# A deformable-convolution block over 32 images: the preparation of the next image on a new table of units

## The chip, the core and the metric

The kernel runs on one core of a Trainium2 chip. The metric is device time in microseconds (us) of one execution. Five engines run their own instruction streams in the order in which the code writes them: PE (TensorE matmul, with its weight loads shown apart as PEld), DVE (VectorE), ACT (ScalarE), POOL (GpSimd) and SP (SyncE, which here only issues DMAs). They meet at semaphores.

## What is computed

The input is 32 images of 192 channels and 32 x 32 pixels. Each goes through two residual blocks, both with a group normalization (`_gn`, 32 groups) in front. The first block is an attention over channels, the second a deformable 3 x 3 convolution, followed by a batch normalization over all images and a gelu:

```python
qkv = jnp.einsum('bnc,dc->bnd', x_flat, w_qkv)
attn = jax.nn.softmax(jnp.einsum('bcn,bdn->bcd', q, k) * SCALE, axis=-1)
out = jnp.einsum('bnc,dc->bnd', jnp.einsum('bcd,bdn->bcn', attn, v).transpose(0, 2, 1), w_out) + b_out
...
offset = jnp.clip(_conv(x, off_w, off_b), -max_off, max_off)      # max_off = 8
mask = 2.0 * jax.nn.sigmoid(_conv(x, mask_w, mask_b))
p = corner(y0i, x0i, ...) + corner(y0i, x0i + 1, ...) + corner(y0i + 1, x0i, ...) + corner(y0i + 1, x0i + 1, ...)
out = jnp.einsum('bckhw,ock->bohw', p, w.reshape(co, c_, K))
...
yn = (y - mean) * jax.lax.rsqrt(var + 1e-05) * gamma + beta
return jax.nn.gelu(yn, approximate=False)
...
x = x + _L0_conv_ref(_gn(x), ...)
x = x + _L1_conv_ref(_gn(x), ...)
```

## The kernel before

**Main work of an image.** The bilinear sampling is done as matmuls. For a tile of 128 output pixels and one kernel row, POOL multiplies a row hat `ay` by a column hat `bx` into a sampling matrix `sT` (L1324, 24 of them per image in a ring of three buffers). An image has 48 units: 8 tiles, 3 kernel rows, 2 chunks of input rows. In unit u, PE turns the matrix of unit u + 2 (`turn_s`, L680, three transposes into `sps`), multiplies sampled by projected pixels for unit u (`convolve`, L697 to L699, nine matmuls), and projects the input for unit u + 10 (`z_group`, L666 to L670, five matmuls into `zps`). In the last ten units these projections, and in the last two the turns, already belong to the next image, as does what POOL makes for them. ACT copies `sps` and `zps` into 16-bit high parts (`sh`, `zh`), and DVE forms what the copies lose (`sl` at L1147, `zl` at L1141). PE waits for `sl` two units later and cannot run further ahead.

**Preparation of the next image.** After its main work in unit u, each engine calls `part0(u, b + 1)`, a hand-written list that places one piece of the next image's preparation in that unit. In the order of the list: statistics of the loaded image (DVE), group statistics (PE, L532 and L533, four matmuls of two columns), group variance (DVE, L990 to L994), the inverse deviation and bias (POOL, L1290 to L1294), normalization (ACT), residue (DVE, L1000, one instruction per channel block), transposes, the attention by a Gram matrix and its small products (L540 among them), the new `x1`, the second normalization into the planes `x2` with their residues, then the shifted planes `x2s` and the seams `x2w` that wrap round the image (`move`, DVE, L1006 to L1010), the offset convolution (PE, L609, 48 matmuls in each of units 38 and 39) and the hats. The group statistics stand in units 4 and 28, POOL's inverse deviations in 5 and 29, residues in 8, 10, 32 and 34, moves in 33, 35 and 36. POOL has fewer pieces of main work, so it calls the list for units 2p - 4 and 2p - 3 after matrix p.

**Loads and stores.** SP stores the finished `x1` of an image, loads the next `x`, and stores `y`, in that order. After the loop over images there is one pass of batch normalization and gelu over all of `y`, about 230 us, that this change does not touch. The loop runs two images per iteration, so that buffers alternate.

Of the kernel before, what the change touches and what calls it, by code (L numbers as in the profile page):

```python
# [35 lines left out]
P = 128  # L36
C, H, W = 192, 32, 32
N = H * W
# [44 lines left out]
def build(nc, x, w_qkT, w_v, w_outT, b_out, w_off, b_off, w_proj, proj_b, gamma, beta,  # L83
# [6 lines left out]
    with ExitStack() as ctx:  # L90
# [59 lines left out]
        x2s = [sb(f"x2s_{n}", [P, 2, PAD_ROWS * W], F16) for n in ("hi_a", "lo_a", "hilo_b")]  # L150

        x2w = [sb(f"x2w_{n}", [P, 2, 2 * WRAP * W], F16) for n in ("hi_a", "lo_a", "hilo_b")]

        x2 = [sb(f"x2_{n}", [P, 2, PAD_ROWS * W], F16) for n in ("hi_a", "lo_a", "hilo_b")]
# [72 lines left out]
        x1_stored = sem("x1_stored")  # L227
        x2_moved = sem("x2_moved")
# [44 lines left out]
        SLOTS = UNITS  # L273
# [58 lines left out]

        def images(program, eng):

            part0, part1, weights_ready = program
            for u in range(SLOTS):
                part0(u, 0, 0)
                if u == 15:  # L340
                    weights_ready()
            part1(0, 0, True)
            with nc.Fori(1, NB - 2, 2, engines=[eng.engine], hint_back_edge=True) as b:
                part1(b, 1, True)
                part1(b + 1, 0, True)
            part1(NB - 1, (NB - 1) % 2, False)

        def image_alone(program, b, i):

            part0, part1, far_pass = program
            for u in range(SLOTS):
                part0(u, b, 0)
            part1(b, 0, False, i)
            far_pass(b, i)
# [7 lines left out]
        AHEAD = 10  # L364
        FAR_SLOT = S_RING - 1
# [49 lines left out]
        def _(sp):  # L415
# [25 lines left out]

            def convolved(b):
                sp.wait_ge(y_final, b + 1)
                store_y(b)

            attended(0)
            with sp.Fori(1, NB - 2, 2) as b:
                attended(b)
                convolved(b - 1)
                attended(b + 1)  # L450
                convolved(b)
            attended(NB - 1, False)
            convolved(NB - 2)


# [18 lines left out]
            def image(b, i):  # L474
                load_x(i)
                sp.wait_ge(x1_sb, 4 * b + 4)
                store_x1(i)
                sp.wait_ge(y_final, b + 1)
                store_y(i)
# [34 lines left out]
        def _(pe):  # L514
# [29 lines left out]
            def transpose_x(r, b):  # L544
                if r == 0:
                    pe.wait_ge(xn_lo, 4 * b + 2)
# [73 lines left out]
            def part0(u, b, par):  # L620
                if u == 4:
                    group_stats(0, b)
                if 12 <= u < 16:
                    transpose_x(u - 12, b)
                if u == 16:
                    gram_product(b)
                if u == 17:
                    gram_times_wq(b)
                if u == 18:
                    pe.wait_ge(t1_sb, b + 1)  # L630
                    square(log_ps, t1, wk, l0[0], C)
                if u == 21:
                    pe.wait_ge(prob_sb, b + 1)
                    square(r_ps, prob, wo, l0[1], C)
                if u == 22:
# [6 lines left out]
                if 23 <= u < 27:  # L642
                    apply_m(u - 23, b)
                if u == 28:
                    group_stats(1, b)
                if 38 <= u < 40:
                    for t in range(TILES // 2):
                        offset_conv(TILES // 2 * (u - 38) + t, b, par)
# [94 lines left out]
            def part1(b, par, more, i=None):  # L743
# [5 lines left out]
                for u in range(UNITS):  # L749
                    if u + 2 < UNITS:  # L750
                        turn_s(u + 2, b)
                    elif more:
                        turn_s(u + 2 - UNITS, b + 1)
                    convolve(u, b, par)
                    if u == 9 and not more and i is None:
# [3 lines left out]
                    elif more:  # L759
                        z_group(u + AHEAD - UNITS, b + 1, 1 - par)  # L760
                    if u % 12 == 2 and u > 12:
                        turn_y(u // 12 - 1, b)
                    if more:
                        part0(u, b + 1, 1 - par)
                turn_y(3, b)
# [7 lines left out]
        def _(act):  # L773
# [13 lines left out]
            def normalize(as_hi, i, src, hi, n, b):  # L787
# [5 lines left out]
                if i == 0:  # L793
# [3 lines left out]
                    if n or not first(b):  # L797
                        act.wait_ge(xn_lo, 4 * b + 2 * n)
# [7 lines left out]
            def part0(u, b, par):  # L806
                if 6 <= u < 10:
                    i = (u - 6) // 2
                    normalize(u % 2, i, xin, (xh_a, xhl_b)[i][:, :], 0, b)
                if 12 <= u < 16:  # L810
                    r = u - 12
# [4 lines left out]
                if u == 17:  # L816
# [4 lines left out]
                if u == 19:  # L821
# [6 lines left out]
                if u == 21:  # L828
                    act.wait_ge(r_ps, b + 1)
                    copy_blocks(rmat, l0[1], C).then_inc(r_sb, 1)  # L830
                if u == 22:
# [4 lines left out]
                if 30 <= u < 34:  # L836
                    if u == 30 and (not isinstance(b, int) or b >= 2):
                        act.wait_ge(sz_done, UNITS * (b - 1))
                    i = (u - 30) // 2
                    normalize(u % 2, i, x1, inner(x2[2 * i], par), 1, b)  # L840
                if u == 41:
                    act.wait_ge(off_sb, b + 1)
                    act.activation(mask[:, par], off[:, par, :, 2 * TAPS:J], ACT.Tanh, scale=0.5)
                if u in (41, 45):
                    h = u // 45
# [5 lines left out]
                if u == 42:  # L851
# [40 lines left out]
            def part1(b, par, more, i=None):  # L892
# [5 lines left out]
                for u in range(UNITS):  # L898
                    if u + 2 < UNITS:
                        split_s(u + 2, b)  # L900
                    elif more:
                        split_s(u + 2 - UNITS, b + 1)
                    if u % 12 == 4 and u < 36:
                        column_hats(u // 12 + 1, b, par)
# [9 lines left out]
                    elif more:  # L914
                        split_z(u + AHEAD - UNITS, b + 1, 1 - par)
                    if more:
                        part0(u, b + 1, 1 - par)
# [18 lines left out]
        def _(dve):  # L936
# [60 lines left out]
            def residue(i, lo, hi, n, b):  # L997

                dve.wait_ge(xn_hi, 4 * b + 2 * n + i + 1)
                dve.tensor_tensor(lo, xn[:, 0] if i == 0 else xn[CB:P, 1], hi, ALU.subtract).then_inc(xn_lo, 1)  # L1000

            def move(k, b, par):

                rows = lambda v: v.rearrange("p (h w) -> p h w", w=W)
# [388 lines left out]
```

## Time and profile before

| | us |
|---|---|
| median of three runs | 3984.57 (3982.10 to 3984.76) |
| profiled execution | 3984.32 |
| its span, first to last instruction | 3982.5 |
| one image in the middle of the loop | 114.3 and 114.8 |

The profile counts, for each engine, the time in which an instruction runs. The trace lists each instruction with its start, its duration and, in square brackets, how long its engine was idle just before it and which engine's instruction released it. "128x512 f16<-128x512 f32" reads: partitions by elements, type, written from read. Two images of an iteration differ by 0.5 us, which stands at the branch that closes the loop.

### The profile page before, as it was taken

What the parts mean: (1) busy time and instruction counts of PE and PEld (TensorE: products, weight loads), DVE (VectorE), ACT (ScalarE), POOL (GpSimd) and SP (SyncE); (2) the same over time, 40 slices, a digit from 0 to 9 for tenths busy, and PEclk for the clock granted to TensorE, in tenths of its full rate; (3) what the DMA queues carried; (4) which work ended last, traced back from release to release, by engine and by line L of the source; (5) the groups of instructions that cost most, each with busy time, mean ns of one, the idle gap of its engine ahead of it and who ended that gap; (6) DMA issues with size and microseconds to landing.
All of it is one profiled execution on the core that took longest, in us unless ns stands there. A gap on an engine that the chain in (4) does not pass through costs nothing.

```text
span 3982.5 us, 108803 instructions
## 1 busy us (share of the span) xinstructions
PE 3538.5 (89%) x38307; PEld 3033.8 (76%) x38307; DVE 2635.5 (66%) x5773; ACT 2105.6 (53%) x4790; POOL 1410.9 (35%) x1165
## 2 busy tenths in 40 slices
PE   3999999999999999999999999999999999999600
PEld 2788888888888888888888888888888888888500
DVE  3567776676677666766776676677766766776522
ACT  1555555555555555655555555555555555555422
POOL 1333333343333333433333333333333433333311
PEclk8999999999999999999999999999999999999855
DMA  2000100001000000000000110000000000000398
GB/s 64 20 10 28 29 28 21 28 28 29 10 29 28 21 28 28 28 17 21 28 29 20 28 28 28 10 28 29 28 21 28 28 28 10 29 28 10 124 356 296
DMA packets 50723, 170.05 MB, mean 43 GB/s; under 512 B 9664, under 2 KB 10880, under 8 KB 50176
## 3 DMA queue, kind: packets, MB, share of 16 engines
q1 hardware_dynamic: 39584, 136.75, 11.4%
q0 software_dynamic: 7168, 25.17, 1.6%
q8 instruction: 336, 5.51, 0.6%
q14 instruction: 211, 1.73, 0.1%
q10 hardware_dynamic: 3424, 0.90, 0.1%
HBM read 87.29 MB, written 75.50 MB: 41 GB/s over the span
## 4 chain that ended last, share of the span: by engine, by line
PE 64%; DVE 14%; issue 9%; ACT 5%; DMA 4%; DVEq 1%; ACTq 1%; SPq 1%; POOL 0%; POOLq 0%
PE sps L680 10%; PE acc L697 6%; PE acc L699 6%; PE acc L698 6%; PE l L609 4%; PE zps L666 3%; PE zps L670 3%; PE zps L668 3%; PE zps L667 3%; PE zps L669 3%; DVE zl L1141 3%; DMA xn<-x_scratch 3%; DVE sl L1147 2%; ACT sh L890 2%; PE l L541 2%
## 5 line engine op out<-in xcount | busy, mean ns | idle before, releaser
L1324 POOL TENSOR_TENSOR sT<-ay,bx 128x768 f32<-128x768 f32 x768 | 1148.0, 1505 | 1334.7 <-PE sps L680 1266.5
L1147 DVE TENSOR_TENSOR sl<-sps,sh 128x384 f16<-128x384 f32 x1536 | 846.3, 551 | 555.6 <-ACT sh L890 552.7
L697 PE MATMUL acc<-zh,sh 128*128 128x192 f16 x4608 | 1133.6, 246 | 0.5 <-ACT ypm L911 0.5
L699 PE MATMUL acc<-zh,sl 128*128 128x192 f16 x4608 | 1133.6, 246 | 0.0
L698 PE MATMUL acc<-zl,sh 128*128 128x192 f16 x4608 | 1133.6, 246 | 0.0
L890 ACT CAST sh<-sps 128x384 f16<-128x384 f32 x1536 | 739.2, 481 | 678.7 <-PE sps L680 669.2
L866 ACT CAST zh<-zps 128x288 f16<-128x288 f32 x1536 | 618.4, 403 | 635.5 <-PE zps L670 608.1
L1141 DVE TENSOR_TENSOR zl<-zps,zh 128x288 f16<-128x288 f32 x1536 | 693.3, 451 | 323.1 <-ACT zh L866 317.2
L680 PE MATMUL sps<-eye,sT 128*128 128x128 f32 x4608 | 784.8, 279 | 110.7 <-DVE sl L1147 96.1
L680 PEld LDWEIGHTS sps<-eye,sT 128*128 128x128 f32 x4608 | 532.0, 141 | 262.8 <-DVE sl L1147 168.8
L698 PEld LDWEIGHTS acc<-zl,sh 128*128 128x128 f16 x4608 | 450.9, 98 | 17.1
L697 PEld LDWEIGHTS acc<-zh,sh 128*128 128x128 f16 x4608 | 450.8, 98 | 1.5 <-DVE sl L1147 0.5
L699 PEld LDWEIGHTS acc<-zh,sl 128*128 128x128 f16 x4608 | 450.9, 98 | 0.0
L666 PE MATMUL zps<-wpr_h,x_hi_a 128*128 128x288 f16 x1344 | 384.5, 286 | 0.8 <-DVE zl L1141 0.3
L670 PE MATMUL zps<-wpr_l,x_hilo_b 128*128 128x288 f16 x1344 | 384.4, 286 | 0.0
L669 PE MATMUL zps<-wpr_h,x_hilo_b 128*128 128x288 f16 x1344 | 384.4, 286 | 0.0
L668 PE MATMUL zps<-wpr_h,x_lo_a 128*128 128x288 f16 x1344 | 384.4, 286 | 0.0
L667 PE MATMUL zps<-wpr_l,x_hi_a 128*128 128x288 f16 x1344 | 384.4, 286 | 0.0
L1308 POOL TENSOR_TENSOR bx<-off,cx_sb 128x576 f32<-128x576 f32 x128 | 155.3, 1214 | 459.1 <-DVE off L1104 459.1
L1290 POOL TENSOR_TENSOR rstd<-gvar,mhalf 128x2 f32<-128x2 f32 x64 | 44.8, 700 | 558.5 <-DVE gvar L994 558.5
L609 PE MATMUL l<-wof,x2s_hi_a 128*128 128x54 f16 x1536 | 182.9, 186 | 9.8 <-DVE x2w_hilo_b L1010 9.8
L609 PE MATMUL l<-wof,x2s_lo_a 128*128 128x54 f16 x1536 | 182.8, 186 | 0.0
(201 smaller groups left out, 6465.7 us busy)
## 6 DMA issues: line engine op xcount, KB each, us to landing
xin<-in_x SPq DMA_DIRECT2D x32, 512.0 KB, 5.5
xin<-in_x SPq DMA_DIRECT2D x64, 256.0 KB, 5.9
x_scratch<-x SPq DMA_DIRECT2D x32, 512.0 KB, 2.7
y_scratch<-ych SPq DMA_DIRECT2D x32, 512.0 KB, 2.7
zh<-y_scratch SPq DMA_DIRECT2D x20, 512.0 KB, 10.9
zl<-x_scratch SPq DMA_DIRECT2D x20, 512.0 KB, 12.1
out<-zh POOLq DMA_DIRECT2D x20, 512.0 KB, 9.1
x_scratch<-x SPq DMA_DIRECT2D x32, 256.0 KB, 3.4
```

The lines of the kernel that those rows point to most:

```text
L609: mm = pe.matmul(o, src[:, row * W:(row + ROWS_T) * W], wof[:, m, k].rearrange("p i j -> p (i j)"), start=(k == 0 and n == 0), stop=(k == ...
L666: pe.matmul(o, at(0), wpr_h[:, 0, ky, n], start=True, stop=False)
L667: pe.matmul(o, at(0), wpr_l[:, 0, ky, n], start=False, stop=False)
L680: mm = pe.transpose(sps[u % 2][:, kx * P:(kx + 1) * P], sT[:, g, kx, c * P:(c + 1) * P], eye32[:, :])
L697: pe.matmul(acc[:, 0:C], s_h, zh[:, j, ky, z], start=start and kx == 0, stop=False)
L698: pe.matmul(acc[:, 0:C], s_h, zl[:, j, ky, z], start=False, stop=False)
L699: mm = pe.matmul(acc[:, 0:C], s_l, zh[:, j, ky, z], start=False, stop=stop and kx == 2)
L866: act.copy(z_piece(zh, g, par), zps[:, g % 2, 0:KO // 2]).then_inc(z_hi, 1)
L890: act.copy(sh[:, u % S_RING].rearrange("p k n -> p (k n)"), sps[u % 2][:, 0:3 * P]).then_inc(s_hi, 1)
L1141: dve.tensor_tensor(z_piece(zl, g, par), zps[:, g % 2, 0:KO // 2], z_piece(zh, g, par), ALU.subtract)\
L1147: dve.tensor_tensor(one(sl), sps[u % 2][:, 0:3 * P], one(sh), ALU.subtract).then_inc(s_lo, 1)
L1324: pool.tensor_tensor(sT[:, p % ST_RING].rearrange("p k (r x) -> p k r x", r=R), a, x_, ALU.mult)\
```

## The change

Each stage of the preparation now has a name, and one table (`PLAN`) gives the unit in which each stands. Units below zero are the last ten of the image before, so an image's preparation begins there, and two images can be in preparation at the same time (`beside` calls the list for `b + 1` and for `b + 2`). The residues are split in two halves of 512 elements, one per unit. The twelve copies of `move` on DVE are replaced by four DMAs that SP issues (`shift`): two seams and two shifted planes, 128 x 3 x 96 and 128 x 3 x 1023 elements. POOL then clears the two edge columns (`edges`). The last turn of `y` moves from the end of an image into unit 1 of the next. Turns of y, column hats and y statistics stand in other units. For the first image the early part of the table is squeezed into 18 units, and more images stand outside the loop.

```diff
+        PLAN = {-10: ("x_stats0", "x_stats1"), -9: ("x_stats2", "x_stats3"), -5: ("moments0",), -3: ("group0",),
+                -2: ("rstd0",), -1: ("norm0",), 0: ("norm1",), 1: ("norm2", "low0"), 2: ("norm3", "low1"),
...
+                21: ("apply3",), 22: ("moments1",), 24: ("group1",), 25: ("rstd1",), 26: ("norm4",),
+                27: ("norm5",), 28: ("norm6", "low4"), 29: ("norm7", "low5"), 30: ("low6",), 31: ("low7",),
+                36: ("edges0",), 38: ("offsets0",), 39: ("offsets1",), 40: ("clip0",), 41: ("rows0",),
...
+        def beside(part0, u, b, par, left):
+            if u < 0:
+                return
+            if left >= 1:
+                for stage in first_plan(u) if first(b) else PLAN.get(u, ()):
+                    part0(stage, b + 1, 1 - par)
+            if left >= 2:
+                for stage in PLAN.get(u - UNITS, ()):
+                    part0(stage, b + 2, par)
...
+            def shift(b, par):
+                sp.wait_ge(xn_lo, 8 * b + 8)
...
+                sp.dma_start(x2w_all[:, :, par, 0:WRAP * W], plane[:, :, N - WRAP * W:N]).then_inc(x2_shifted, 16)
...
+                sp.dma_start(flat_plane(0)[:, :, 1:N], plane[:, :, 0:N - 1]).then_inc(x2_shifted, 16)
...
-            def move(k, b, par):
-                rows = lambda v: v.rearrange("p (h w) -> p h w", w=W)
-                src = rows(inner(x2[k], par))
-                dve.tensor_copy(rows(inner(x2s[k], 0))[:, :, 1:W], src[:, :, 0:W - 1])
...
+            def edges(b):
+                pool.wait_ge(x2_shifted, 64 * b + 64)
...
+                    for u in (2 * p - 4, 2 * p - 3):
+                        beside(part0, u, b, par, left)
+                for u in range(UNITS - 4, UNITS):
+                    beside(part0, u, b, par, left)
```

**POOL, end of an image and start of the next.** Before, the column distances for the next image (L1308) and the last matrix of this one are followed straight by the next image's first three matrices; the inverse deviation comes between matrices 4 and 5:

```order
L1306 REGISTER_ALU
L1308 TENSOR_TENSOR bx<-off,cx_sb 128x576 [waits off_sb]
L1320 ISA
L1324 TENSOR_TENSOR sT<-ay,bx 128x768 [waits s_ps]
L1316 ISA
L1318 ISA [waits hats]
L1320 ISA [waits bx_made]
L1324 TENSOR_TENSOR sT<-ay,bx 128x768 [waits s_ps]
L1320 ISA
L1324 TENSOR_TENSOR sT<-ay,bx 128x768 [waits s_ps]
```

After, the three instructions of `rstd0` for the image after the next stand there, with a wait for the group variance:

```order
L1345 REGISTER_ALU
L1347 TENSOR_TENSOR bx<-off,cx_sb 128x576 [waits off_sb]
L1318 ISA
L1319 TENSOR_TENSOR rstd<-gvar,mhalf 128x2 [waits gn_var]
L1320 ISA
L1321 TENSOR_TENSOR nbias<-gmv,rstd 128x2 [waits gn_rstd]
L1322 ISA
L1323 TENSOR_TENSOR nbias<-nbias,minus 128x2 [waits gn_mean]
L1355 ISA
L1357 ISA [waits hats]
L1359 ISA [waits bx_made]
L1363 TENSOR_TENSOR sT<-ay,bx 128x768 [waits s_ps]
```

What moved: the inverse deviation now stands ahead of the next image's first matrix.

**PE, around the group statistics of the first normalization.** Before, in unit 4, the four small matmuls are followed by a turn that needs no new matrix:

```order
L532 MATMUL l_0<-mv,avg_sb 128x2 [waits gn_stats]
L533 MATMUL l_0<-mv,avg_sb 128x2
L532 MATMUL l_0<-mv,avg_sb 128x2
L533 MATMUL l_0<-mv,avg_sb 128x2
L677 ISA
L680 MATMUL sps<-eye,sT 128x128 [waits s_lo]
```

After, in unit 45, the turn behind them is the next image's first and waits for its matrix (`st_made`):

```order
L719 MATMUL zps<-wpr_l,x 128x288
L579 ISA
L582 MATMUL l_0<-mv,avg_sb 128x2 [waits gn_stats]
L583 MATMUL l_0<-mv,avg_sb 128x2
L582 MATMUL l_0<-mv,avg_sb 128x2
L583 MATMUL l_0<-mv,avg_sb 128x2
L724 ISA
L726 ISA [waits st_made]
L729 MATMUL sps<-eye,sT 128x128 [waits s_lo]
```

What moved: four small matmuls, to a place just ahead of a wait for POOL.

**DVE, residues of the second normalization.** Before, a whole residue and the four copies of a plane alternate with the two instructions that feed PE (`sl`, `zl`):

```order
L1000 TENSOR_TENSOR x_lo_a<-xn,x_hi_a 128x1024 [waits xn_hi]
L1145 ISA
L1147 TENSOR_TENSOR sl<-sps,sh 128x384 [waits s_hi]
L1140 ISA
L1141 TENSOR_TENSOR zl<-zps,zh 128x288 [waits z_hi]
L1083 REGISTER_ALU
L1006 COPY x2s_hi_a<-x_hi_a 128x32x31 [waits off_ps]
L1007 COPY x2s_hi_a<-x_hi_a 128x32x31
L1009 COPY x2w_hi_a<-x_hi_a 128x96
L1010 COPY x2w_hi_a<-x_hi_a 128x96
```

After, each unit holds one half of a residue and no copy:

```order
L1053 TENSOR_TENSOR x<-xn,x 128x512 [waits xn_hi]
L1172 ISA
L1174 TENSOR_TENSOR sl<-sps,sh 128x384 [waits s_hi]
L1167 ISA
L1168 TENSOR_TENSOR zl<-zps,zh 128x288 [waits z_hi]
L1051 ISA
L1053 TENSOR_TENSOR x<-xn,x 128x512 [waits xn_hi]
```

The copies' work left DVE and went to DMAs in SP's queue.

## Rows read from the trace of the kernel before

**Rows 1.** Page, busy time by engine; shares of the chain that ended last.

```profile
PE 3538.5 (89%) x38307; PEld 3033.8 (76%) x38307; DVE 2635.5 (66%) x5773; ACT 2105.6 (53%) x4790; POOL 1410.9 (35%) x1165
...
PE 64%; DVE 14%; issue 9%; ACT 5%; DMA 4%; DVEq 1%; ACTq 1%; SPq 1%; POOL 0%; POOLq 0%
```

**Rows 2.** Windows, two images: us, busy of PE, PEld, DVE, ACT, POOL, clock, DMA.

```profile
1951.80:2066.60 114.80, 110.25 (x1200) 94.50 (x1198) 80.69 (x180) 63.80 (x148) 42.77 (x35) 1.00 0.09 25
2066.60:2180.90 114.30, 110.03 (x1200) 94.56 (x1198) 79.59 (x178) 63.83 (x148) 42.46 (x34) 1.00 0.08 25
```

**Rows 3.** Waits of image 2066.6 to 2180.9: total us, times, longest.

```profile
PEld sps L680 <- DVE sl L1147: 5.6, 7, 1.4
...
PEld l L540 <- DVE gram L1057: 0.9, 1, 0.9
...
PEld l L532 <- DVE mv L984: 0.5, 1, 0.5
```

**Rows 4.** Timeline of PEld, units 33 to 45 of one image: start, us.

```profile
2032.61 0.31 PEld L680 LDWEIGHTS sps<-eye,sT 128*128 128x128 f32 x3 [0.44 <-DVE sl L1147]
...
2035.59 0.31 PEld L680 LDWEIGHTS sps<-eye,sT 128*128 128x128 f32 x3 [1.39 <-DVE sl L1147]
...
2037.80 0.32 PEld L680 LDWEIGHTS sps<-eye,sT 128*128 128x128 f32 x3 [0.61 <-DVE sl L1147]
...
2040.78 0.31 PEld L680 LDWEIGHTS sps<-eye,sT 128*128 128x128 f32 x3 [1.38 <-DVE sl L1147]
2042.09 0.10 PEld L666 LDWEIGHTS zps<-wpr_h,x_hi_a 128*128 128x128 f16 x1 [0.25 <-issue]
...
2057.86 0.31 PEld L680 LDWEIGHTS sps<-eye,sT 128*128 128x128 f32 x3 [0.92 <-DVE sl L1147]
...
2059.86 0.20 PEld L680 LDWEIGHTS sps<-eye,sT 128*128 128x128 f32 x2 [0.40 <-DVE sl L1147]
```

**Rows 5.** Timeline of DVE, same units; line L1000 (min/median/max ns).

```profile
2030.38 1.72 DVE L1000 TENSOR_TENSOR x_lo_a<-xn,x_hi_a 128x1024 f16<-128x1024 f32 x1
...
2033.53 1.45 DVE L1009 COPY x2w_hi_a<-x_hi_a 128x96 f16<-128x96 f16 x1
...
2041.69 0.17 DVE L1009 COPY x2w_hilo_b<-x_hilo_b 128x96 f16<-128x96 f16 x1
...
L1000 DVE TENSOR_TENSOR x_lo_a<-xn,x_hi_a x32: 1225/1714/1717, 90.0 to 3633.9; 128x1024 f16<-128x1024 f32 x32
```

**Rows 6.** Timeline, unit 4 of an image, group statistics; line L1324 (min/median/max ns).

```profile
2075.49 0.38 PE L533 MATMUL l<-mv,avg_sb 64*128 64x2 f32 x2
...
2076.79 0.70 POOL L1290 TENSOR_TENSOR rstd<-gvar,mhalf 128x2 f32<-128x2 f32 x1 [5.70 <-DVE gvar L994]
...
2077.99 2.91 POOL L1324 TENSOR_TENSOR sT<-ay,bx 128x768 f32<-128x768 f32 x2
...
L1324 POOL TENSOR_TENSOR sT<-ay,bx x768: 1468/1479/1697, 107.6 to 3736.8; 128x768 f32<-128x768 f32 x192
```

**Rows 7.** Timeline of PE ahead of the first image; windows there, columns as rows 2.

```profile
104.07 0.29 PE L670 MATMUL zps<-wpr_l,x2w_hilo_b 128*128 128x288 f16 x1
109.78 0.42 PE L666 MATMUL zps<-wpr_h,x2w_hi_a 128*128 128x288 f16 x1 [5.42 <-DVE zl L1141]
...
103.60:107.00 3.40, 0.76 (x7) 0.37 (x4) 2.08 (x10) 2.10 (x5) 1.43 (x1) 1.00 0.01 2
107.00:113.80 6.80, 4.02 (x17) 2.29 (x18) 2.69 (x9) 2.78 (x8) 5.68 (x4) 0.50 0.00 0
```

**Rows 8.** Page, DMA: queue totals; a store (us to landing); timeline of SP, load.

```profile
q1 hardware_dynamic: 39584, 136.75, 11.4%
...
y_scratch<-ych SPq DMA_DIRECT2D x32, 512.0 KB, 2.7
...
2019.65 2.15 SPq L418 DMA_DIRECT2D xin<-in_x  x3
```

More of the change, by code:

```diff
@@ L741, in far_pass, with part1 @@
                     mm.then_inc(fyt_ps, 1)
-            def part1(b, par, more, i=None):
+            def part1(b, par, left, i=None):
                 if first(b) or i is not None:
@@ L751, in part1 @@
                         turn_s(u + 2, b)
-                    elif more:
+                    elif left:
                         turn_s(u + 2 - UNITS, b + 1)
                     convolve(u, b, par)
-                    if u == 9 and not more and i is None:
+                    if u == 9 and not left and i is None:
                         offset_max(b)
@@ L758, in part1 @@
                         z_group(u + AHEAD, b, par)
-                    elif more:
+                    elif left:
                         z_group(u + AHEAD - UNITS, b + 1, 1 - par)
[L761 to L765, printed above, removed]
+                    if u in TURN_Y:
+                        turn_y(TURN_Y.index(u), b)
+                    if u == TURN_LAST_Y and not first(b) and i is None:
+                        turn_y(3, b - 1)
+                    beside(part0, u, b, par, left)
+                if not left:
+                    turn_y(3, b)
             wq, wk = wqk[:, :, 0:C], wqk[:, :, C:2 * C]
@@ L1224, in part1 @@
                         split_s(u + 2, b)
-                    elif more:
+                    elif left:
                         split_s(u + 2 - UNITS, b + 1)
@@ L1294, in group_rstd, with part0 @@
                 pool.tensor_tensor(nbias[:, :], nbias[:, :], minus[:, :], ALU.mult).then_inc(gn_bias, 1)
-            def part0(u, b, par):
-                if u == 5:
-                    group_rstd(0, b)
-                if u == 29:
-                    group_rstd(1, b)
-                if u == 41:
-                    column_distance(0, b, par)
+            def part0(stage, b, par):
+                name, q = stage[:-1], int(stage[-1])
+                if name == "rstd":
+                    group_rstd(q, b)
+                if name == "edges":
+                    edges(b)
+                if name == "columns":
+                    column_distance(0, b, par)
+            def edges(b):
+                pool.wait_ge(x2_shifted, 64 * b + 64)
+                pool.sem_inc(edges_due, 1)
+                for h in range(2):
+                    rows = x2s_all[:, :, h, PAD_T * W:PAD_T * W + N].rearrange("p k (r w) -> p k r w", w=W)
+                    ins = pool.memset(rows[:, :, :, (W - 1) * h:(W - 1) * h + 1], 0.0)
+                ins.then_inc(x2_moved, 1)
             def column_distance(q, b, par):
@@ L1327, in part1 @@
                         column_distance((1, 4, 10).index(p) + 1, b, par)
-                    if more:
-                        for u in (2 * p - 4, 2 * p - 3):
-                            part0(u, b + 1, 1 - par)
+                    for u in (2 * p - 4, 2 * p - 3):
+                        beside(part0, u, b, par, left)
+                for u in range(UNITS - 4, UNITS):
+                    beside(part0, u, b, par, left)
             images((part0, part1, lambda: None), pool)
```

246 lines of the change are left out of this document (125 added, 121 removed), and 4 rows, old and new, of the table PLAN.

## The prediction

> **What bounds the kernel now.** I read four views, from coarse to fine. The page first: PE is busy 89% of the span, DVE 66%, ACT 53%, POOL 35%, and 64% of the chain that ended last is PE, 14% DVE [rows 1]. PE is the bound, so only time in which PE stands still can be won, and any new wait of PE is paid in full. Next the windows of two images in the middle: 114.80 and 114.30 us, mean 114.55, with PE busy 110.25 and 110.03 and the granted clock 1.00, the upper of its two levels, 2.4 GHz [rows 2]. The gap of about 4.4 us is a lower bound of what can be won, since a busy PE is modelled and small waits hide in it. Then the waits of one image, PE's weight loads (PEld), which are the first of PE to stand still: 5.6 us in seven waits of the turns (L680) for DVE's `sl`, 0.9 us of the product `prob x wo` (L540) for DVE, and 0.5 us of the group statistics (L532) for DVE's moments [rows 3]. Last, where the seven waits stand: four of 0.44, 1.39, 0.61 and 1.38 us in units 33 to 37, and two of 0.92 and 0.40 us behind the clipping and the row hats in units 43 to 45 [rows 4]. The four fall on the units in which DVE runs the second normalization's residues and the copies, and the two longest follow seam copies of 1.45 us, which take 0.17 us when nothing disturbs them [rows 5]. A residue takes 1.72 us in the middle case and 1.22 us at the least [rows 5].
>
> The row shows a copy of 96 elements at 1.45 us, just what is left of one POOL matrix of 1.48 us [rows 5, 6]. The Trainium skill's page "SBUF — State Buffer", section "SBUF: two separate sides", says that VectorE and GpSimd share one pair of ports as an exclusive lock, so that the later one stands still for the other's whole instruction; it says so too of a VectorE operation with two SBUF inputs. By that rule a half residue can still meet a matrix, and the split would win less than the halved duration suggests.
>
> **The change, part by part.** All per image; 30 images of the loop have both a preparation beside them and a neighbour.
>
> *Copies and whole residues leave DVE's long units: a gain.* The turns' waits are 5.6 us in all. The two of 0.92 and 0.40 us stay, because clip, rows and row hats keep units 40 to 46. So 5.6 - 1.3 = 4.3 us goes, the first normalization's residue wait among it. The attention chain is spread by one unit more (from `exp` to `prob_wo` in 13 to 16, before 19 to 21), which takes the 0.9 us of L540. The moments now stand two units ahead of the statistics (43 to 45, 22 to 24), which takes the 0.5 us of L532. The last turn of `y` leaves the end of the image, and the projection in unit 38 (L666) stood 0.25 us behind the planes [rows 4]: 0.25 us. Sum: 4.3 + 0.9 + 0.5 + 0.25 = -5.95 us.
>
> *What the halves leave.* Beside `sl` and `zl`, about 1.0 us of a unit of 1.7, DVE has some 0.7 us free. A half is 1.22 / 2 = 0.61 us, or more if it meets a matrix: a whole residue shows 1.72 - 1.22 = 0.5 us of that [rows 5]. Eight halves in eight units, of which a few run over: 0 to 1.2 us, I take +0.6, nearest to one such collision in full.
>
> *Four DMAs and the edges instead of copies.* The copies cost PE only through DVE, and that is counted. The new chain is: last half residue (unit 31), SP's issues, transfers, POOL's two memsets, and then PE's projection for the next image in unit 38, which waits for `x2_moved`. SP spends 2.15 us on three issues, 0.72 us each [rows 8]; the two seams go first, 1.4 us. The bytes are 2 x 128 x 3 x (96 + 1023) x 2 = 1.72 MB. The queue moved 136.75 MB in 11.4% of 16 engines' span, 136.75 / (0.114 x 3982.5) = 0.301 MB per us [rows 8], so 5.7 us. A store of 512 KB lands after 2.7 us [rows 8], of which 1.7 us is bytes at that rate, so 1.0 us is fixed. The memsets I put at 0.6 us. Sum 1.4 + 5.7 + 1.0 + 0.6 = 8.7 us. The time for it: the first residue of before starts at 2030.38 in unit 32 and the projection stands at 2042.09 [rows 4, 5], 11.7 us, less the four waits of 3.8 us, is 7.9 us; the last half starts a unit (1.7 us) earlier and takes 0.7 us or more and DVE's lag, so 7.5 to 8.5 us. I take 7.9, so PE waits 8.7 - 7.9 = +0.8 us, from 0 to 3 us (if the transfers, beside a load, take half as long again). SP waits there with the store of `y` behind it, and that store has until unit 16 of the next image; nobody waits. POOL waits for the DMAs in `edges` with the matrix of units 42 and 43 behind it, which has four units; nobody waits unless it is over 3 us.
>
> That transfer can be priced by the skill too. The page "DMA: Bandwidth & Descriptors", section "Anatomy of one DMA — SWDGE (gpsimd) path", fits about 2.0 us plus bytes / 436e3: an estimate of 5.9 us for the 1.72 MB in place of 6.7. It is a fit for another way of issuing, and by it PE would not wait in unit 38, and the forecast would be 24 us less.
>
> *The inverse deviation ahead of the next image's first matrix: the largest term.* Before, POOL computes `rstd` in unit 5, between matrices 4 and 5, with three matrices in its ring ahead of PE; it waits 5.7 us there, and nobody waits for it [rows 6]. After, the order has `rstd0` of the image after the next behind the last matrix, with the next image's first matrix queued behind it on POOL. It waits for DVE's variance, and that waits for PE's four small matmuls at the end of unit 45. PE's next instruction, at the start of unit 46, is the next image's first turn, and it waits for just that matrix. So PE, DVE, POOL and PE again form a chain with nothing beside it, and ACT and DVE, fed by PE, run dry behind it. Its price stands in the trace: the last small matmul ends at 2075.49 + 0.38 = 2075.87, `rstd` runs from 2076.79, and the matrix behind it starts at 2077.99 and lasts 1.48 us, until 2079.47 [rows 6]. That is 3.6 us. The hand-over back to PE comes on top, and DVE may be late by one `sl` as it now stands behind the row distances of unit 44: 3.6 to 4.5 us, I take +3.9, the lower part, since PE's wait lets DVE catch up.
>
> The same table puts `rstd1` in unit 25, behind the matrix of units 28 and 29 and one unit after the statistics, with four units until the next matrix is wanted: no cost. Nor has the attention such a chain, as its POOL part is nil.
>
> *The clock after that stall.* Ahead of the first image PE stood still for 5.42 us, from 104.36 to 109.78, and the granted clock was 0.50, the lower level of 1.2 GHz, from 107.0 to 113.8: 6.8 us with PE busy 4.02 us [rows 7]. The work of 4.02 us at the lower level takes half as long at the upper, so the fall cost 2.0 us. In the loop, where no wait of PE is over 1.4 us, the clock stayed at 1.00 [rows 2, 4]. The new stall of 3.9 us lies between these, nearer to the long one. I take +2.0 us, with 0 (no fall) and 3.4 us (the whole 6.8 us at half speed) as ends.
>
> The row shows the fall after a pause. The page "TensorE: Matmul & The Clock Gate", section "Why this matters for your kernels", asks for no idle gaps between bursts of matmuls, or the clock drops to its lower level; this speaks against the change, by its rule the forecast stands, and without it the first rival below.
>
> *Once.* The first image's offsets wait for DMAs (8.7 us) instead of DVE's copies (about 3.6 us), and its neighbour's early stages are squeezed into 18 units: +8 us, 0 to 20.
>
> **Sum.** -5.95 + 0.6 + 0.8 + 3.9 + 2.0 = +1.35 us per image, 30 x 1.35 = 40.5, +8: 48.5 us above the profiled execution's 3984.32 (span 3982.5 and 1.8 around it), which is 0.25 below the median of 3984.57. Forecast **4033 us**. Its own range goes with the ends that are likely together (stall and clock 5.0 to 7.3 in place of 5.9, halves 0 to 1.2): 3998 to 4085.
>
> **Rivals.** *The clock does not fall* (faster). The stall of 3.9 us is shorter than the one that the trace shows, and small matmuls and late transposes may count as work. Then -0.65 per image: 3984.3 - 19.5 + 8 = 3973 us, from 3941 to 3995. It decides at a clock loss of 0.4 us per image, (5.95 - 5.3) less the 8 us once. *The DMAs come late.* If they share with a load and take 3 us too long: +2.2 more per image, 4099 us; for it speaks that rate per byte is an average of large stores and loads, against it that nothing else is due then. *The stall is hidden.* If POOL's matrix were made before PE comes, 3.9 and 2.0 fall away: -4.55 per image, 3856 us. Against it stands the order of POOL's instructions; it needs PE to run late by four units, which no row shows. *The change does not win what it says*: halves run over and the waits stay, half of the 4.3 us stays: +2.1 per image, 4096 us.
>
> **How the numbers follow.** Forecast 62%, no fall 20%, DMAs late 9%, stall hidden 5%, waits stay 4%. The range must leave out no more than 2 in 10: from 3960 (two thirds of the second case stay in) to 4095 (most of the forecast's upper end, about half of the late ones). A measurement of this kernel tells about 0.2%, 8 us, from no change: 3976 to 3992. Faster: the hidden stall, and three quarters of no fall, 5 + 15 = 20%, and 1% of the forecast: 21%. Same: the rest of no fall and the lowest of the forecast, 13%. Slower: 66%.
>
> **What would show it.** In the changed profile: (1) in the timeline of PEld, once per image, a wait of the turn L729 for POOL's `sT` of 3.6 to 4.5 us, right after L583, with POOL's L1319 in it; (2) windows after it with a granted clock below 1.00, and PE's clock in the page's slices below 9 or the mean below before's; (3) no wait of L729 over 0.5 us in units 1 to 5 and 28 to 33; (4) at the projection L715 in unit 38 a wait for POOL's memset L1340 of 0 to 3 us. The prediction is wrong if (1) is missing or below 2 us, and my size of the clock term is wrong if images with the stall show 1.00 throughout.

## The result and the profile after

The changed kernel takes **4041.61 us** in the median (4037.25 to 4046.26, four runs) against 3984.66 us for the kernel before on the same chip. The ratio is 1.0144, with a 95% interval from 1.0127 to 1.0162: 57 us or 1.4% slower, where 4033 us was forecast. The span of the profiled execution is 4035.5 us.

The page after, the same two parts as in [rows 1]: busy time of the engines, and the shares of the chain that ended last.

```profile
PE 3538.2 (88%) x38307; PEld 3088.6 (77%) x38307; DVE 2500.6 (62%) x5517; ACT 2101.5 (52%) x4790; POOL 1416.7 (35%) x1225
...
PE 61%; issue 14%; DMA 9%; POOL 6%; DVE 4%; ACT 3%; SPq 2%; POOLq 0%; DVEq 0%; ACTq 0%
```

DVE has 135 us less to do, as meant. But its share of the chain went from 14% to 4% while POOL's, nil before, became 6%, DMA's went from 4% to 9% and "issue" from 9% to 14%. PE's busy time is as before: what it lost it spent waiting, as the next views show. Two images in the middle (windows, counted from 0 these are images 16 and 17; columns as in [rows 2]):

```profile
1990.40:2107.10 116.70, 109.70 (x1200) 96.00 (x1198) 75.46 (x171) 63.80 (x149) 42.68 (x36) 0.99 0.12 39
2107.10:2222.50 115.40, 110.25 (x1199) 96.48 (x1197) 76.07 (x171) 63.63 (x149) 42.84 (x37) 0.97 0.13 40
```

An image takes 116.05 us in the mean where it took 114.55, and the granted clock is no longer 1.00. The waits of the first of them, total us, times and longest, as in [rows 3]:

```profile
PEld sps L729 <- issue: 5.7, 5, 4.7
PE sps L729 <- POOL sT L1363: 4.6, 1, 4.6
...
PEld zps L715 <- issue: 1.3, 1, 1.3
PEld sps L729 <- DVE sl L1174: 1.3, 2, 0.9
...
PE zps L715 <- POOL x2s L1340: 1.1, 1, 1.1
...
PEld acc L746 <- ACT ypm L963: 0.8, 1, 0.8
```

The turn's seven waits of 5.6 us for `sl` are down to two of 1.3 us, the two behind the clipping and the row hats. In their place stands one wait of 4.6 us of the turn for POOL's matrix (the line with 4.7 us that is put down to "issue" is the same stall, seen by the weight loads), and two that are smaller: the projection in unit 38 for POOL's memset, and the convolution behind unit 29 for ACT's copy of its sums (`ypm`). The large one stands once per image at the start of unit 46. Here it is in the timeline of image 16; columns as in [rows 6], the lines that [rows 6] answers to among them:

```profile
2096.89 0.38 PE L583 MATMUL l<-mv,avg_sb 64*128 64x2 f32 x2
2097.02 0.55 DVE L1174 TENSOR_TENSOR sl<-sps,sh 128x384 f16<-128x384 f32 x1
...
2097.49 0.45 DVE L1168 TENSOR_TENSOR zl<-zps,zh 128x288 f16<-128x288 f32 x1
...
2097.86 0.15 DVE L1041 COPY gmv<-l 128x4 f32<-128x4 f32 x1
...
2098.56 0.70 POOL L1319 TENSOR_TENSOR rstd<-gvar,mhalf 128x2 f32<-128x2 f32 x1 [8.56 <-DVE gvar L1045]
...
2099.61 0.20 POOL L1323 TENSOR_TENSOR nbias<-nbias,minus 128x2 f32<-128x2 f32 x1
2100.25 2.91 POOL L1363 TENSOR_TENSOR sT<-ay,bx 128x768 f32<-128x768 f32 x2 [0.44 <-issue]
...
2101.87 0.90 PE L729 MATMUL sps<-eye,sT 128*128 128x128 f32 x3 [4.59 <-POOL sT L1363]
```

Read it downward: the small matmuls end at 2097.27; DVE still has `sl` and `zl` to do and takes the group's numbers at 2097.86; POOL's three instructions and its matrix follow, and PE starts 4.59 us after it stopped. In the next image the small matmuls end at 2212.89 and the same round is shorter:

```profile
2213.09 0.15 DVE L1041 COPY gmv<-l 128x4 f32<-128x4 f32 x1
...
2215.14 2.91 POOL L1363 TENSOR_TENSOR sT<-ay,bx 128x768 f32<-128x768 f32 x2
...
2216.76 0.90 PE L729 MATMUL sps<-eye,sT 128*128 128x128 f32 x3 [3.88 <-POOL sT L1363]
```

DVE is 0.20 us behind PE instead of 0.59, and POOL goes on to its matrix without the 0.44 us. Through the loop the stall is 4.6 and 3.9 us in turn, 4.25 us in the mean of images 2 to 28.

The three transposes behind it take 0.90 us, where a turn takes 0.55. The windows around the stall of image 16 show why (columns as in [rows 2]):

```profile
2097.30:2101.80 4.50, 0.00 (x0) 0.00 (x0) 1.03 (x5) 0.72 (x2) 2.64 (x5) 0.97 0.00 0
2101.80:2105.10 3.30, 3.23 (x18) 2.77 (x19) 0.56 (x1) 0.48 (x1) 3.30 (x3) 0.53 0.00 0
2105.10:2108.50 3.40, 3.40 (x37) 3.18 (x35) 2.53 (x7) 2.86 (x7) 2.05 (x2) 1.00 0.03 7
```

After the stall the clock is at its lower level for 3.3 us, in which PE runs 18 matmuls where it runs 37 in the 3.4 us behind. Such a fall stands at this place in every image from 0 to 29, for 3.4 or 6.8 us.

### The profile page after: what moved, and what is told of

Read it like the earlier page. It is cut to its first block, busy times and chain, and to the rows that moved or that the text cites. A ratio compares the mean times of both kernels' runs of the same rounds, so it can differ in the third digit from the quotient of the medians.

```text
span 4035.5 us, 107978 instructions
## 1 busy us (share of the span) xinstructions
PE 3538.2 (88%) x38307; PEld 3088.6 (77%) x38307; DVE 2500.6 (62%) x5517; ACT 2101.5 (52%) x4790; POOL 1416.7 (35%) x1225
## 4 chain that ended last, share of the span: by engine, by line
PE 61%; issue 14%; DMA 9%; POOL 6%; DVE 4%; ACT 3%; SPq 2%; POOLq 0%; DVEq 0%; ACTq 0%
PE sps L729 10%; PE acc L746 7%; PE acc L747 7%; PE acc L748 7%; DMA x2s<-x 4%; POOL sT L1363 4%; PE zps L715 3%; PE zps L716 3%; PE zps L717 3%; PE zps L718 3%; PE zps L719 3%; DMA xn<-x_scratch 2%; PE l L591 2%; DMA out<-x 1%; PE l L590 1%
## 5 line engine op out<-in xcount | busy, mean ns | idle before, releaser
L746 PE MATMUL acc<-zh,sh 128*128 128x192 f16 x4608 | 1147.6, 249 | 18.0 <-ACT ypm L963 18.0
L747 PE MATMUL acc<-zl,sh 128*128 128x192 f16 x4608 | 1146.3, 249 | 0.5 <-issue 0.5
L748 PE MATMUL acc<-zh,sl 128*128 128x192 f16 x4608 | 1145.6, 249 | 0.0
L729 PEld LDWEIGHTS sps<-eye,sT 128*128 128x128 f32 x4608 | 554.4, 143 | 256.0 <-issue 156.2
L715 PE MATMUL zps<-wpr_h,x 128*128 128x288 f16 x1344 | 389.4, 290 | 14.7 <-POOL x2s L1340 14.3
L716 PE MATMUL zps<-wpr_l,x 128*128 128x288 f16 x1344 | 389.2, 290 | 0.0
L717 PE MATMUL zps<-wpr_h,x 128*128 128x288 f16 x1344 | 389.1, 290 | 0.0
L718 PE MATMUL zps<-wpr_h,x 128*128 128x288 f16 x1344 | 388.6, 289 | 0.0
L719 PE MATMUL zps<-wpr_l,x 128*128 128x288 f16 x1344 | 387.7, 288 | 0.0
L659 PE MATMUL l<-wof,x2s 128*128 128x54 f16 x4608 | 186.7, 186 | 16.4 <-POOL x2s L1340 16.4
L659 PEld LDWEIGHTS l<-wof,x2s 128*128 128x128 f16 x4608 | 180.8, 96 | 19.6 <-POOL x2s L1340 16.5
```

The costliest lines, as they stand in the source:

```text
L715: pe.matmul(o, at(0), wpr_h[:, 0, ky, n], start=True, stop=False)
L716: pe.matmul(o, at(0), wpr_l[:, 0, ky, n], start=False, stop=False)
L717: pe.matmul(o, at(1), wpr_h[:, 0, ky, n], start=False, stop=False)
L729: mm = pe.transpose(sps[u % 2][:, kx * P:(kx + 1) * P], sT[:, g, kx, c * P:(c + 1) * P], eye32[:, :])
L746: pe.matmul(acc[:, 0:C], s_h, zh[:, j, ky, z], start=start and kx == 0, stop=False)
L747: pe.matmul(acc[:, 0:C], s_h, zl[:, j, ky, z], start=False, stop=False)
```

## Experiments

Two theories stood at the start. The first is that of the prediction: DVE got its relief, and a new chain through POOL at the end of each image, with the clock behind it, costs more than that. The rival: the waits are DVE's and only change their place when stages are moved.

**The statistics three units earlier.** The whole round (moments, small matmuls, inverse deviation) starts three units ahead of the turn that waits for POOL's matrix. All else stays as in the changed kernel.

```diff
-   ... -5: ("moments0",), -3: ("group0",), -2: ("rstd0",), ...
+   ... -8: ("moments0",), -6: ("group0",), -5: ("rstd0",), ...
```

> One change to the changed kernel: the moments, group statistics and inverse deviation of the first normalization stand three units earlier (units 40, 42 and 43 in place of 43, 45 and 46 of the image before); PE then has units 43 to 45, some 6.2 us of work with their waits, between its small matmuls and the turn that needs POOL's matrix. Theory (the stall of 4.6 us and the clock fall behind it, some 1.5 us, are the loss): both vanish, 31 x 6.1 = 190 us less than 4041.6, about 3853 us, and the granted clock is 1.00 through the loop. Rival (stall counts, clock does not): 31 x 4.6, about 3899 us. Rival (DVE, already late behind clip and hats in units 40 to 44, only moves the wait there): between 3920 and 4040 us, with new waits of the turn or of the group statistics in units 42 to 44.

Measured: 3890.71 us, 0.9759 of before (0.9736 to 0.9783). That is 151 us less than the changed kernel, and 2.4% faster than the kernel before. The loop in one window, and the waits of two images in its middle, 2027.3 to 2137.7 and the one before it, 1914.7 to 2027.3:

```profile
500.00:3500.00 3000.00, 2926.98 (x32276) 2555.88 (x32274) 2068.60 (x4585) 1714.67 (x3988) 1163.39 (x972) 1.00 0.13 41
```

```profile
PEld sps L729 <- DVE sl L1174: 0.9, 2, 0.5
...
PEld l L582 <- DVE mv L1035: 0.6, 1, 0.6
...
PE sps L729 <- POOL sT L1363: 0.6, 1, 0.6
```

```profile
PEld sps L729 <- DVE sl L1174: 2.6, 3, 1.4
...
PE zps L715 <- POOL x2s L1340: 1.4, 1, 1.4
...
PE sps L729 <- POOL sT L1363: 1.1, 1, 1.1
```

The stall is down to 0.6 and 1.1 us in turn and the clock is 1.00. Not all of the 190 us came, since 2.5 us of smaller waits for DVE and POOL now stand in units 42 to 45, where the changed kernel has 1.15 us beside its stall: the rival that DVE's waits only change their place is right for a fifth of the gain. By its time alone the run would also fit the other rival, by which the clock costs nothing (3899 us); the run with work inside the stall, below, separates the two.

**The statistics one unit earlier** (the same edit with -6, -4 and -3): does a shorter stall keep the clock?

> As the changed kernel, but moments, group statistics and inverse deviation stand one unit earlier (42, 44 and 45). PE has one unit, 1.7 us, between the small matmuls and the turn that waits for POOL's matrix, so the stall should shrink from 4.6 to 2.3 to 2.9 us. Theory that the clock falls only behind a long stall: 31 x (2.0 + 1.5) less than 4041.6, about 3933 us, and the clock at 1.00. Theory that any stall of over 2 us makes it fall: 31 x 2.0 less, about 3980 us, and a granted clock in the loop as low as in the changed kernel.

Measured: 3969.68 us (0.9954 of before, 0.9932 to 0.9976). The last small matmul and the next turn that waits for POOL, and the window behind that turn's start:

```profile
2064.44 0.38 PE L583 MATMUL l<-mv,avg_sb 64*128 64x2 f32 x2
...
2069.47 0.54 PE L729 MATMUL sps<-eye,sT 128*128 128x128 f32 x3 [2.82 <-POOL sT L1363]
```

```profile
2070.00:2074.00 4.00, 4.00 (x28) 3.48 (x26) 2.07 (x7) 1.35 (x3) 4.00 (x4) 0.58 0.01 4
```

The stall is 2.82 us here and 2.46 us in the next image, and so on in turn. The clock still falls, in every image from 2 to 27; images 1, 28 and 29, with stalls of 2.47, 2.44 and 2.18 us, show no fall. Of the eight executions the shortest (3951 us) has a mean clock of 0.960 and the longest (3986 us) one of 0.954, so the number of falls seems to differ between them. The median is 10 us below what the second theory gave and 37 us above the first.

**Work inside the stall**, to see the clock alone: the changed kernel with matmuls that nobody reads.

```diff
                 if name == "group":
                     group_stats(q, b)
+                    for _ in range(24 if q == 0 else 0):
+                        pe.matmul(l0[1][:, 0:KO // 2], wpr_h[:, 0, 0, 0:P], wpr_h[:, 0, 0, 0:KO // 2],
+                                  start=True, stop=True)
```

> The changed kernel with 24 more matmuls of 288 columns behind the small matmuls of unit 45, whose results nobody reads: 24 x 0.12 = 2.9 us of work inside PE's stall of 4.6 us. Theory (the clock falls because PE does nothing, and costs 1.5 us per image): the granted clock is 1.00 in the loop, the stall for POOL's matrix shows as 1.2 to 2 us behind the added matmuls, and the time is 31 x 1.5 = 46 us less than 4041.6, about 3995 us. Rival (the slow stretch after the stall is the refilling of ACT and DVE, not the clock): no change, 4030 to 4050 us.

Measured: 3971.96 us (0.9971 of before, 0.9960 to 0.9982), 70 us less than the changed kernel although PE does more. The loop, and the turn behind the added matmuls:

```profile
500.00:3500.00 3000.00, 2934.74 (x32095) 2560.29 (x32091) 1990.36 (x4476) 1676.49 (x3901) 1127.03 (x943) 1.00 0.13 40
```

```profile
2066.26 0.54 PE L732 MATMUL sps<-eye,sT 128*128 128x128 f32 x3 [1.55 <-POOL sT L1366]
```

The clock stays at 1.00, POOL's matrix comes as late as ever, and an image is 2.3 us shorter. So the fall is a cost of its own, and not a refilling of ACT and DVE: behind the stall units 46 and 47 take 1.68 us each, as any unit without extra work. In the mean of images 2 to 28 the two kernels differ in four units alone: 45 (0.3 us, the slow turn), 46 (1.4 us), 47 (0.1 us) and 38 (0.5 us). The last is not the clock, since the wait for the DMAs is nearly gone in this kernel (see the last section). That leaves 1.8 us for the clock.

**DVE's copies in place of the DMAs**, on the kernel with the statistics three units earlier: `shift` and `edges` out, the old `move` in units 33, 35 and 36.

```diff
-   36: ("edges0",), ...
+   33: ("move0",), 35: ("move1",), 36: ("move2",), ...
```

> As the run with the statistics three units earlier, but the shifted planes and seams are copied by DVE again, in units 33, 35 and 36, in place of the four DMAs and POOL's clearing of edge columns; residues stay in halves at units 28 to 31. Theory (the copies were most of the 3.5 us that PE waited in units 33 to 37): the waits of the turn behind the two locked seam copies come back, 1.5 to 2.6 us per image, less the 0.7 us that PE waits for the DMAs in unit 38: 30 to 60 us slower than the run with the DMAs. Rival (the residues made those waits, the copies alone fit in the units): 20 us faster than it, since the wait in unit 38 is gone.

Measured: 3942.27 us (0.9892 of before, 0.9869 to 0.9914), 52 us slower than with the DMAs. Two seam copies in the timeline, with POOL's matrix beside each, and the turn's waits of one image:

```profile
2129.97 1.54 POOL L1384 TENSOR_TENSOR sT<-ay,bx 128x768 f32<-128x768 f32 x1 [1.69 <-PE sps L732]
...
2130.09 1.47 DVE L1066 COPY x2w<-x 128x96 f16<-128x96 f16 x1
...
2134.82 1.55 POOL L1384 TENSOR_TENSOR sT<-ay,bx 128x768 f32<-128x768 f32 x1 [3.31 <-PE sps L732]
...
2134.96 1.45 DVE L1065 COPY x2w<-x 128x96 f16<-128x96 f16 x1
```

```profile
PEld sps L732 <- DVE sl L1195: 3.3, 4, 1.2
```

Each long seam copy ends within 0.1 us of the matrix that runs beside it, and PE waits in units 35 and 37 again.

**Whole residues**, on the same kernel: one instruction of 1024 elements in the unit of the second half.

```diff
-                i, half = q // 2, slice(q % 2 * (N // 2), (q % 2 + 1) * (N // 2))
+                if q % 2 == 0:
+                    return
+                i, half = q // 2, slice(0, N)
...
```

> As the run with the statistics three units earlier, but each residue is one instruction again, at the place of its second half (units 2, 4, 29 and 31). Theory (a whole residue beside the two instructions that feed PE is longer than a unit): a wait of the turn of 0.3 to 0.5 us behind each, 1.2 to 2.0 us per image, 35 to 60 us slower than with halves. Rival (DVE's slack over several units hides it): within 10 us of the run with halves.

Measured: 3907.58 us (0.9808 of before, 0.9783 to 0.9832). That is 17 us slower than with halves, between the theory and its rival, and hardly clear of noise: the interval with halves ends at 0.9783, where this one begins. The waits that appear are in units 4 and 6; the larger one:

```profile
2261.14 0.31 PEld L729 LDWEIGHTS sps<-eye,sT 128*128 128x128 f32 x3 [0.43 <-DVE sl L1176]
```

By units, whole residues cost 0.5 us per image in units 4 to 6, behind the first normalization, and nothing behind the second. In the traces 0.3 us of that is offset by shorter waits in units 38 and 44.

**What is left**, one at a time on the same kernel. First, DVE's units 40 to 46 are thinned:

```diff
-   ... 44: ("rows1",), 45: ("row_act1",), 46: ("row_hats1",)}
+   ... 54: ("rows1",), 55: ("row_act1",), 57: ("row_hats1",)}
...
-   ... -9: ("x_stats2", "x_stats3"), -8: ("moments0",), ...
+   ... -9: ("x_stats2", "x_stats3", "moments0"), ...
```

Units 54, 55 and 57 are 48 + 6, 7 and 9: they lie in the image that uses the hats, and `beside` now calls the table for them too.

> As the run with the statistics three units earlier (3890.7 us), with DVE's units 40 to 46 thinned: the second half of the row distances and hats moves into units 6, 7 and 9 of the image that uses them, and the moments of the first normalization stand in unit 39. Theory (PE's waits of 0.5, 0.3, 0.6 and 1.0 us in units 42 to 45 come from DVE, which has more there than fits): 1.6 to 2.2 us less per image, 3822 to 3841 us. Rival (the waits follow the instructions into units 6 to 9): within 15 us of 3891.

Measured: 3853.97 us (0.9665, 0.9647 to 0.9683), 37 us less, though short of the 3822 to 3841 of the theory: the waits of units 42 and 43 are gone, that of unit 45 stayed (0.9 us). Second, the second normalization two units earlier:

```diff
-   21: ("apply3",), 22: ("moments1",), 24: ("group1",), 25: ("rstd1",), 26: ("norm4",), ... 31: ("low7",), 36: ("edges0",),
+   21: ("apply3", "moments1"), 22: ("group1",), 23: ("rstd1",), 24: ("norm4",), ... 29: ("low7",), 34: ("edges0",),
...
```

> As the run with the statistics three units earlier (3890.7 us), with the second normalization two units earlier (moments 21, statistics 22, POOL 23, ACT 24 to 27, residues 26 to 29), the edges in 34, the third column hats in 20, the second turn of y in 28. Theory (ACT's four normalizations end too near to its copy of the sums at unit 29, 0.74 us, and the DMAs start too late for unit 38, 0.66 us): both waits vanish, 1.4 us per image, about 3847 us. Rival (the DMAs are slow because of what else moves, not late): the wait in unit 38 stays, about 3868 us.

Measured: 3899.56 us (0.9789, 0.9773 to 0.9806): nothing gained. Both waits went, and as much came back: the small matmuls wait in unit 22 for DVE's moments (1.0 us of the weight loads), which the next kernel shows too. Third, both together:

> The last two together. If their waits are independent, 3.0 to 3.6 us per image less than 3890.7 us: 3780 to 3800 us. If DVE's load around units 26 to 31 or 6 to 9 makes new waits, 3800 to 3850 us.

Measured: 3852.78 us (0.9678, 0.9662 to 0.9694), the same as the first alone, where 3780 to 3800 us stood to be won without new waits. The small matmuls' wait in one image:

```profile
PEld l L585 <- DVE mv L1038: 1.0, 1, 1.0
```

So two units were one too many. Next, the same kernel with the second normalization one unit earlier than in the change instead of two, and the first normalization's statistics in unit 41:

> As the run with both later row hats and earlier normalization, but that normalization one unit earlier only (moments 22, statistics 23, POOL 24, ACT 25 to 28, residues 27 to 30, edges 35), since two units made PE wait 1.1 us for DVE's moments in unit 22; and the first normalization's statistics in unit 41, POOL in 42. Theory: against the run with the later row hats alone (3854 us) the waits of 0.74 us in unit 29, some 0.5 us in unit 38 and 0.6 us for POOL's matrix in unit 45 go, 1.8 us per image, about 3797 us, PE's waits of an image under 2.5 us in all. Rival (the statistics one unit earlier make PE wait for DVE, late behind the clipping, in unit 41): 3815 to 3850 us.

Measured: 3834.76 us (0.9626, 0.9604 to 0.9648). The wait for POOL in unit 45 is gone, but in 10 of images 2 to 28 there is a new one of 1.7 us in unit 37, and the 3797 us of the theory were missed. POOL and PE in such an image:

```profile
1743.73 0.94 POOL L1343 MEMSET x2s<- 128x96 f16 x2 [9.71 <-DMA x2s<-x]
```

```profile
1746.00 0.54 PE L732 MATMUL sps<-eye,sT 128*128 128x128 f32 x3 [1.66 <-POOL sT L1366]
```

POOL stood in `edges`, waiting for the DMAs, with PE's next matrix queued behind it. The ten are just the images in which the DMAs land 9.0 us after the first issue, and not 7.1 to 7.4 (last section). Two ways on from there: POOL's inverse deviation one unit earlier still, and `edges` behind one more matrix.

> As the run before, with the statistics in unit 40 and POOL's inverse deviation in 41, now between the last two matrices of the image. Theory (unit 41 is early enough): within 8 us of the run before. Rival (DVE's lag from the clipping still reaches POOL's matrix in unit 45): 10 to 20 us faster. Rival (DVE runs clip and group variance in the same unit and PE waits behind it): 10 to 30 us slower.

Measured: 3867.17 us (0.9703, 0.9679 to 0.9728), 32 us slower: PE waits 1.4 us in unit 44. The timeline of one image, from POOL to the wait of PE's weight loads:

```profile
1995.81 0.69 POOL L1322 TENSOR_TENSOR rstd<-gvar,mhalf 128x2 f32<-128x2 f32 x1 [10.86 <-DVE gvar L1048]
...
1999.81 0.69 ACT L912 ACTIVATE bx<-bx 128x576 f32<-128x576 f32 x1 [0.98 <-POOL bx L1350]
...
2001.64 0.56 DVE L1177 TENSOR_TENSOR sl<-sps,sh 128x384 f16<-128x384 f32 x1 [1.28 <-ACT sh L945]
...
2002.25 0.31 PEld L732 LDWEIGHTS sps<-eye,sT 128*128 128x128 f32 x3 [1.49 <-DVE sl L1177]
```

This is the mechanism of the change once more. POOL waits for the variance with a matrix and the column distances `bx` queued behind it; so `bx` is late, ACT stands still for it ahead of its next `sh`, DVE waits for `sh`, and PE for `sl`.

> As the run with the statistics in unit 41, with POOL's edges one unit later (36 in place of 35), behind one more matrix. There the DMAs' slower images (9.1 us from the first issue to the memset against 7.4) held POOL, and PE waited 1.7 us for POOL's next matrix in unit 37. Theory: that wait goes and the projection of unit 38 waits at most a few tenths, 0.5 to 0.8 us per image less, 3810 to 3820 us. Rival (the wait moves whole to the projection in unit 38): 3825 to 3840 us.

Measured: **3805.99 us**, 0.9547 of before (0.9527 to 0.9567): 4.5% faster than the kernel before, and 5.8% than the changed one. Its loop:

```profile
500.00:3500.00 3000.00, 2983.78 (x33159) 2629.03 (x33159) 2073.06 (x4696) 1755.58 (x4088) 1179.72 (x998) 1.00 0.13 42
```

An image takes 108.24 us. The kernel has the table, the halves, the DMAs and the late turn of `y` of the change; only units differ, with the call of the table for units from 48 on.

## Why the prediction was right, step by step

For the sizes per unit I took the distance from the first `convolve` matmul of a unit to that of the next, as a mean over images 2 to 28 (counted from 0), in both kernels. What a unit takes without a wait is read from units with the same work elsewhere: 1.68 us as such, 2.88 us with the four small matmuls. "Forecast" is the prediction's term.

| per image, us | forecast | measured | from |
|---|---|---|---|
| turns' waits for `sl` gone | -4.3 | -3.9 | units 34 to 37: 3.46, units 10 and 12: 0.48 |
| `prob x wo` | -0.9 | -0.9 | its unit, 4.48 to 3.61 |
| second group statistics | -0.5 | -0.4 | its unit, 3.29 to 2.88 |
| end of image, unit 38's old wait | -0.25 | -0.7 | units 47 and 38: 0.54 and 0.20 |
| halves run over | +0.6 | 0.0 | units 1 to 4 and 28 to 33, but for ACT's wait in 29 |
| DMAs late for unit 38 | +0.8 | +0.6 | unit 38, 1.2 and nothing in turn |
| stall for POOL's matrix | +3.9 | +4.25 | unit 45 with the clock at 1.00, 1.73 to 7.18, less 1.2 of small matmuls |
| clock behind it | +2.0 | +1.8 | units 45 to 47, against the kernel with work in the stall |
| ACT's copy late, unit 29 | none | +0.7 | unit 29 |
| units 5 and 6 | none | +0.1 | the same units |
| sum | +1.35 | +1.55 | whole images, 114.54 to 116.09 |

The profiled executions differ by 53.0 us: 43.5 us in images 1 to 28, and 9.5 us once, where +8 was forecast. Of the latter, the first image starts 7.9 us later and takes 7.2 us more, and images 29 to 31 with the pass behind them give 5.5 us back. The medians differ by 57 us, since the profiled execution of the changed kernel is the shortest of its four.

- **The mechanism of the largest term was right**, and the order of the instructions gave it away: POOL's wait placed ahead of the matrix that PE needs next. The runs with the statistics moved show that its place is what costs. Its size was 3.9 for 4.25: in every second image the stall is the 3.9 us of the forecast, in the others 4.6, above the stated 3.6 to 4.5, because `sl` and `zl` of unit 45 stand in front of the group's numbers (0.6 us from the small matmuls' end in place of 0.2) and POOL shows 0.44 us more before its matrix. Why the images take turns is not shown.
- **The clock** fell as forecast, so the first rival did not happen, and the run with work inside the stall shows it as a cost apart. 2.0 us was taken from one fall ahead of the first image; here it is 1.8. That the two are so near is partly luck, since one fall of 6.8 us stood for falls of 3.4 and 6.8 us.
- **The gain** was right in sum and nearly in its parts, and the run with DVE's copies shows the DMAs as its larger share: 52 us, against 17 us for halves.
- **The halves** were mis-sized, 0.6 for nothing. That the transposes and other long units near by let DVE catch up is my reading; no run shows it.
- **The DMAs**: 8.7 us were worked out from issue to edges done; the times from the first issue to the memset are 7.4 and 8.4 to 9.7 us in turn. A mean of 0.6 us so near to 0.8 is luck: one image waits 1.2 us and the next not at all, and the prediction had nothing that tells them apart (last section).
- **One step was missing**: the table moves ACT's normalizations from units 30 to 33 into 26 to 29, and three of them, of 1.24 to 1.27 us, now stand straight ahead of its copy of the sums in unit 29, for which PE waits 0.7 us. I followed DVE, POOL, SP and PE past the new places, and not ACT.
- **The other rivals**: the stall was not hidden, the waits did go, and the DMAs were not 3 us late.

The forecast's 4033 is thus near 4041.6 partly because errors cancel: per image, the terms that came out dearer make 1.7 us, and those that came out cheaper 1.5 us.

## What to carry to other kernels

When stages are moved by a table, read for each engine what stands behind each wait at its new place: a short instruction that waits for a round through three engines is free with a full ring of finished work behind it, and costs the whole round when it stands directly ahead of the one buffer that the bounding engine needs next. Place the first link of such a round early enough for its full length plus the lag of the engines in it: here three units left 0.6 and 1.1 us of the stall, four left nothing, and five put POOL's wait in front of other work that PE needed. Where PE stalls, look behind the stall for a lower clock, and price it too. Then move one stage at a time: two units were too many for one normalization and one was right, and an edit that gains nothing can be one that trades two waits for a third.

## What the runs showed of the hardware that was not expected

- The granted clock fell to its lower level behind stalls of 2.46 to 2.86 us as it did behind 3.9 and 4.6 us, and cost as much (1.5 us in units 46 and 47 in both kernels). I had expected the short one to be free. The stalls of 0.6 and 1.1 us at the same place left none.
- The length of the stall alone does not tell. In the kernel with the second normalization two units earlier, the clock fell in 7 of images 1 to 29 behind a wait of 0.7 to 0.8 us that four matmuls of two columns follow. One of them, and the windows around it:

```profile
2189.45 0.38 PE L582 MATMUL l<-mv,avg_sb 128*128 128x2 f32 x2 [0.71 <-DVE mv L1035]
```

```profile
2189.00:2192.10 3.10, 2.65 (x23) 2.52 (x24) 1.92 (x8) 0.65 (x2) 0.47 (x1) 1.00 1.01 274
2192.10:2195.50 3.40, 3.40 (x20) 2.79 (x18) 1.35 (x3) 1.31 (x4) 3.24 (x5) 0.50 0.93 272
```

In the kernel with the added matmuls, one turn in image 29 waits 2.71 us for DVE and the clock stays at 1.00. What else decides is open.

- Matmuls without use inside a stall of PE made the kernel faster by 70 us, some 55 us of it by the clock.
- The four DMAs of 1.72 MB, between places of the same memory, landed 7.3 us after the first issue in every second image of the changed kernel and after 8.3 to 9.5 us in the others. The queues tell the two apart (queue, packets, MB, busy share): first image 16, from 2066.7 to 2075.8, then image 17, from 2183.6 to 2190.9.

```profile
q1 hardware_dynamic: 1600, 1.72, 52.9%
q8 instruction: 1, 0.02, 1.2%
```

```profile
q1 hardware_dynamic: 1600, 1.72, 68.2%
```

In image 16 a packet of 16 KB of the instruction queue (q8) runs among them. So it is in all 14 slow images from 2 to 28, and in none of the 13 fast ones. It is not the turn of the images: with the statistics in unit 41 and the edges in 35, ten even images have that packet among their DMAs, which land after 9.0 us, and the four others have not and land after 7.1 to 7.4. With the second normalization two units earlier it falls among the DMAs in no image, and all land after 7.1 to 7.3 us. No run moves the packet alone, so that it is the cause is likely and not proven.
